# Letting the second pair of sequences join an expert loop one visit later, with its steps spread wider

## What is computed

```python
x = _layernorm(x + attention(x, wq, bq, wk, bk, wv, bv, wo, bo))   # 16 heads of 16
x = _layernorm(x + recurrence(x, ctx_1024, w, u))                  # a decaying scan over the 128 tokens
x = _layernorm(x + experts(x, Wg, W1, b1, W2, b2))                 # 8 experts, 256 -> 1024 (gelu) -> 256
```

## Time and profile before

| | us |
|---|---|
| median of 3 runs (lowest, highest) | 917.84 (917.34, 917.88) |
| profiled execution, its own time | 918.12 |
| span of the trace | 916.4 |
| TensorE busy | 876.4 (96% of the span) |
| VectorE busy | 586.0 (64%) |
| ScalarE busy | 576.5 (63%) |
| mean granted TensorE clock | 0.988 of full speed |
| DMA engines, mean rate | 202 GB/s |

### The profile page before, as it was taken

The page is one execution under the profiler, slowest core; times in us unless marked ns, Lnnn a source line. Parts: engine busy times, 40 slices in busy tenths (PEclk is TensorE's granted clock), DMA queues, the critical chain, the costliest instruction groups (busy, mean ns, idle before and its releaser), DMA issues.

```text
span 916.4 us, 17611 instructions
## 1 busy us (share of the span) xinstructions
PE 876.4 (96%) x6547; PEld 797.0 (87%) x6547; DVE 586.0 (64%) x1197; ACT 576.5 (63%) x969; POOL 80.4 (9%) x116
## 2 busy tenths in 40 slices
PE   6898888999999999999999999999999999999997
PEld 6788787889888999989988889889999889999997
DVE  6779798767656576665565674665676564333574
ACT  7568686766667455776557465765557665444684
POOL 4220012001010011000120010200120000000000
PEclk9999899999999999999999999999999999999999
DMA  8459999997738854686548954497537855665340
GB/s 250 154 191 338 352 311 312 285 301 244 240 109 244 242 174 132 178 231 212 174 127 230 235 169 146 134 231 239 181 118 181 250 183 169 190 187 177 103 139 12
DMA packets 195379, 185.00 MB, mean 202 GB/s; under 512 B 61896, under 2 KB 161504, under 8 KB 195296
## 3 DMA queue, kind: packets, MB, share of 16 engines
q1 hardware_dynamic: 195296, 183.88, 66.6%
HBM read 135.60 MB, written 35.65 MB: 187 GB/s over the span
## 4 chain that ended last, share of the span: by engine, by line
PE 76%; ACT 9%; DVE 5%; issue 2%; DMA 2%; SPq 1%; POOL 1%; POOLq 0%; ACTq 0%; DVEq 0%
PE down_ps L823 11%; PE down_ps L824 11%; PE down_ps L825 11%; PE up_ps L562 11%; PE up_ps L564 11%; PE up_ps L563 11%; DMA pt_lo<-p_lo 2%; ACT h_all L971 2%; PE bank L609 1%; ACT probs L912 1%; PE bank L584 1%; ACT L971 1%; PE bank L562 1%; PE bank L564 1%; PE bank L563 1%
## 5 line engine op out<-in xcount | busy, mean ns | idle before, releaser
L971 ACT ACTIVATE h_all<-up_ps,b_all 128x512 f32<-128x512 f32 (+1 forms) x296 | 182.3, 631 | 259.1 <-PE up_ps L564 250.0
L823 PE MATMUL down_ps<-w_hi,h_hi 128*128 128x256 f32 x1024 | 294.4, 288 | 4.4 <-DVE acc L1252 4.4
L1051 DVE TENSOR_TENSOR h_lo<-h_all,h_hi 128x512 fp32r<-128x512 f32 x256 | 176.3, 691 | 191.1 <-ACT h_hi L962 190.5
L824 PE MATMUL down_ps<-w_lo,h_hi 128*128 128x256 f32 x1024 | 289.8, 283 | 0.0
L825 PE MATMUL down_ps<-w_hi,h_lo 128*128 128x256 f32 x1024 | 289.7, 283 | 0.0
L562 PE MATMUL up_ps<-x2t_hi,w_hi 128*128 128x512 f32 (+1 forms) x588 | 220.1, 374 | 3.7 <-DVE x2t_lo L1051 1.9
L564 PE MATMUL up_ps<-x2t_hi,w_lo 128*128 128x512 f32 (+1 forms) x588 | 215.4, 366 | 0.0
L563 PE MATMUL up_ps<-x2t_lo,w_hi 128*128 128x512 f32 (+1 forms) x588 | 214.7, 365 | 0.0
L823 PEld LDWEIGHTS down_ps<-w_hi,h_hi 128*128 128x128 f32 x1024 | 195.1, 190 | 12.9 <-issue 3.0
L824 PEld LDWEIGHTS down_ps<-w_lo,h_hi 128*128 128x128 f32 x1024 | 195.9, 191 | 7.0
L825 PEld LDWEIGHTS down_ps<-w_hi,h_lo 128*128 128x128 f32 x1024 | 195.8, 191 | 0.0
(11 more groups left out here) (213 smaller groups left out, 953.9 us busy)
## 6 DMA issues: line engine op xcount, KB each, us to landing
w_hi<-w_parts SPq DMA_DIRECT2D x200, 256.0 KB, 3.3
w_lo<-w_parts SPq DMA_DIRECT2D x200, 256.0 KB, 3.5
w_raw<-in_w_dram SPq DMA_DIRECT2D x96, 256.0 KB, 4.1
w_parts<-w_hi SPq DMA_DIRECT2D x64, 256.0 KB, 4.0
w_parts<-w_lo SPq DMA_DIRECT2D x64, 256.0 KB, 4.2
x_in<-in_x_dram SPq DMA_DIRECT2D x8, 256.0 KB, 4.1
ctx_sb<-in_ctx_dram SPq DMA_DIRECT2D x8, 256.0 KB, 3.8
out_dram<-acc SPq DMA_DIRECT2D x8, 256.0 KB, 2.3
```

What stands on the lines that cost most here:

```text
L823: nc.tensor.matmul(ps, hi, w2h[:, c, :], start=c == 0 and j == 0, stop=False, skip_group_check=True)
L824: nc.tensor.matmul(ps, hi, w2l[:, c, :], start=False, stop=False, skip_group_check=True)
L971: a = nc.scalar.activation(h_all[:, unit % HALL, k * wide:(k + 1) * wide], up_ps[unit % 2][:, k * wide:(k + 1) * wide], ACT.Gelu_apprx_tan ...
L1051: return nc.vector.tensor_tensor(dst, src, hi.bitcast(F32), ALU.subtract)
```

## The change

Two tables of numbers. Joins move from (0, 5, 9, 13, ...) to (0, 6, 10, 14, ...), so that there are 38 visits instead of 37. The single visits are now 0 to 5, 8 and 9, and the last four; the number of items stays 512. The second pair has 8 more items before it joins and its steps are spread over them. The third pair still joins at item 92, but begins 8 items later. Steps of the later pairs keep their items.

```diff
-JOIN = (0, 5, 9, 13, 17, 21, 25, 29)
+JOIN = (0, 6, 10, 14, 18, 22, 26, 30)
...
 EARLY = [
-    {E_0: 3, E_1: 3, X_BIAS: 6, T_0: 7, T_1: 8, W_0: 10, W_1: 11, S_2: 13, M_2: 13, S_3: 13, M_3: 13, E_2: 15, E_3: 15, T_2: 17, T_3: 18, W_2: 20, W_3: 21,
-     ATT: 22, CTX: 22, WO: 23, NORM1: 25, Y1: 26, XEXP: 26, REC_0: 27, REC_1: 28, REC_2: 29, REC_3: 29, BACK: 31, NORM2: 32, R_TURN: 34,
...
+    {E_0: 3, E_1: 3, X_BIAS: 7, T_0: 8, T_1: 9, W_0: 12, W_1: 13, S_2: 15, M_2: 15, S_3: 15, M_3: 15, E_2: 18, E_3: 18, T_2: 20, T_3:
+     21, W_2: 24, W_3: 25, ATT: 27, CTX: 27, WO: 28, NORM1: 30, Y1: 32, XEXP: 32, REC_0: 33, REC_1: 34, REC_2: 35, REC_3: 35, BACK: 38,
+     NORM2: 39, R_TURN: 42, R_LOGITS: 44, R_MAX: 45, R_GATE: 49, R_GATE_T: 53, R_BIAS: 55},
```

More of the change, by code:

```diff
@@ L1424 @@
 EARLY = [
-    {E_0: 3, E_1: 3, X_BIAS: 6, T_0: 7, T_1: 8, W_0: 10, W_1: 11, S_2: 13, M_2: 13, S_3: 13, M_3: 13, E_2: 15, E_3: 15, T_2: 17, T_3: 18, W_2: 20, W_3: 21,
-     ATT: 22, CTX: 22, WO: 23, NORM1: 25, Y1: 26, XEXP: 26, REC_0: 27, REC_1: 28, REC_2: 29, REC_3: 29, BACK: 31, NORM2: 32, R_TURN: 34,
[L1427 to L1431, removed]
+    {E_0: 3, E_1: 3, X_BIAS: 7, T_0: 8, T_1: 9, W_0: 12, W_1: 13, S_2: 15, M_2: 15, S_3: 15, M_3: 15, E_2: 18, E_3: 18, T_2: 20, T_3:
+     21, W_2: 24, W_3: 25, ATT: 27, CTX: 27, WO: 28, NORM1: 30, Y1: 32, XEXP: 32, REC_0: 33, REC_1: 34, REC_2: 35, REC_3: 35, BACK: 38,
+     NORM2: 39, R_TURN: 42, R_LOGITS: 44, R_MAX: 45, R_GATE: 49, R_GATE_T: 53, R_BIAS: 55},
+    {X: 33, X_LOW: 34, X_BIAS: 35, QK: 37, K_COPY: 37, Q_COPY: 37, K_LOW: 38, Q_LOW: 40, DIAG_0: 41, V: 40, V_ADD: 43, V_SPLIT: 44,
+     S_0: 46, M_0: 46, S_1: 46, M_1: 46, DIAG_1: 48, E_0: 49, E_1: 49, T_0: 51, T_1: 53, S_2: 56, M_2: 56, S_3: 56, M_3: 57, W_0: 60,
+     E_2: 60, E_3: 60, W_1: 61, T_2: 62, T_3: 64, W_2: 67, W_3: 69, ATT: 71, CTX: 72, WO: 73, NORM1: 75, Y1: 77, XEXP: 77, REC_0: 77,
+     REC_1: 78, REC_2: 79, REC_3: 80, BACK: 84, NORM2: 85, R_TURN: 87, R_LOGITS: 89, R_MAX: 90, R_GATE: 91, R_GATE_T: 95, R_BIAS: 97}]
 LAG = 3
```

## The result

The changed kernel takes 922.85 us (median of 8 runs, 920.11 to 927.51), the kernel before 917.86 in the same session: a ratio of 1.0052, 95% interval 1.003 to 1.0073. It is **slower by 0.5%**, where 913.5 us was forecast, in a range up to 920.5.

What follows compares the result with a forecast made beforehand. The prediction took TensorE as the bound nearly everywhere, with VectorE's backlog making it wait and full DMA engines right behind in the single visits. Its eight terms summed to -4.3 us, from 918.1 to a median of 913.5 us, range 907 to 920.5.

Steps and rivals of the forecast that it cites:

- term 6: Third pair: W_2 and W_3 come too close behind T_2 and T_3 for their transposes, +1.1 us (0 to 2.2).
- the first rival: Single visits: DMA engines take the gain, or full VectorE only moves its waits; 917.4 us, no difference; chance 0.19.
- Term 8: Single visits, items 10 to 49: DMA needs 5.9 us from slack, mostly held by 8.3 us in hand; +2.0 (0 to 6.6).
- the second's: Rival: late kept copies delay the third pair's transposes, W_3 waits 8.2 us and a dip follows; 921 us, chance 0.18.
- Term 5: Two 2.0 us waits of down items for `acc`: unchanged at the join, gone at visit 5's end, -2.0 (0 to -2.0).
- Term 3: After the second pair's ATT wait: the 5.6 us clock dip to 0.50 goes, -2.5 us (0 to -2.5).
- term 2: Second pair's ATT: TensorE's 4.0 us wait falls to 1.2, -2.8 us (bounds -1.4 and -4.0).
- term 4: BACK: its 1.7 us wait for `mix` nearly goes with one more item between, -1.3 us (0 to -1.7).
- term 7: Visits 8 and 9: reads of kept weights may make TensorE wait anew, +0.5 us (0 to 3).
- Term 1: One double visit becomes two single ones with more, narrower matmuls on TensorE, +0.7 us.

Runs made afterwards that it cites:

- all_three: Changed kernel with kept copies and reads halved, third pair's W_2 and W_3 at items 68 and 71, BACK and NORM2 at 82 and 83: 914.62 us, 0.9959.
- before_half: Kernel before with every kept copy and every read of a kept part cut to half its columns: ratio 0.9992 to the kernel before.
- after_half: Changed kernel with kept copies and reads cut to half their columns: ratio 0.9997 to the kernel before.
- spaced: Changed kernel, full copies, third pair's W_2 and W_3 at 68 and 71, REC_3 at 80, BACK at 83, NORM2 at 84: 918.43 us, 1.0002.
- after_w23: Changed kernel with the third pair's W_2 and W_3 at items 68 and 71, ATT to REC_3 up to two items later: 921.07 us, 1.0034.

## Why the prediction was wrong

**The sum, in three parts.** The forecast was -4.3 us, the measured +0.52% are +4.8. The halved and spaced versions split the difference of 9.1, each part good to some 2 us:

| part | forecast | measured | from |
|---|---|---|---|
| terms 1 to 5, the later joins and the wider spacing | -7.9 | -3.0 | `all_three` less `before_half` |
| term 6 and what it left out, the third pair's table | +1.1 | +3.5 | `after_half` less `all_three` |
| terms 7 and 8, the DMA traffic | +2.5 | +4.3 | changed kernel less `after_half`, less the 0.7 that halving gives the kernel before |

The largest miss is in the first part.

**Terms 2 to 5 were counted whole.** They took 8.6 us off, as if a wait that goes were time won. In `all_three`, with the traffic halved and the third pair spaced, waits are only 3.0 and the clock 1.0 below the kernel before. ATT gave 2.2 and one wait for `acc` 2.0. The wait of the join for `x2t_lo`, put at 0, went from 1.9 to 0.5. Against that `xt_lo` (projections) is waited for 1.4 more, gelu 1.0 and BACK 1.0, and a wait of 1.0 for `x` (L1237) is new. From 80.1 to 156.2 us VectorE is busy for 67.8 of 76.1 us there, against 63.8 in the halved kernel before. This is near what the first rival said in its last sentence, that VectorE only moves its waits; that its fullness is the cause is argued, not shown.

**Term 8 and the rivals.** The step that failed here is "That holds the 5.9, though not at each piece: +2.0"; the traffic cost 4.3. The slack of one piece, 8.3 us, was taken for that of all. It wasn't: other pieces had 2.5 and 5.3 in hand already before, in the changed kernel the copies were up to 12 us late, and ScalarE waited for them 12.2 us in all. Of the changed kernel's ledger, the halved one lacks 2.3 us of gelu's wait, 2.0 of the join's, 0.7 of the transposes' and 3.6 of clock, 8.6 us together, in an execution that was 4.7 above the median. That ScalarE's splits would wait for copies was the first rival's mechanism, and copies that delay the transposes the second's, at 0.18 and 921 us; it measured 922.85. That 921 is near is luck in part. The point against it, that slower items would give the transposes time, was true only in part: the wait for `pt_lo` was 4.1 us, not 8.2, and the rest came through gelu and the join, which it didn't have.

**Term 5.** The wait at the end of the double visit went, as forecast. The one at the join was put at 0 change ("the same steps around it now") and grew by 2.0. ScalarE there waited 3.7 us for a copy, and VectorE got its pieces late. The halved kernel has it at 2.0, so that the growth goes with the traffic.

**Term 6** had mechanism and sign right: +1.1 forecast; 3.4 us of wait with halved copies, 4.1 in full. It went wrong by taking half the bound, and even the bound of 2.2 was too low.

**A term was missing.** Pairs leave at the end of visit 7, and that end moved from item 90 to item 82, in front of BACK and NORM2. The additions, the moments and R_TURN's late `x2`, on VectorE after the change:

```profile
228.78 1.65 DVE L1252 SCALAR_TENSOR_TENSOR acc<-down_ps,gate,acc 128x256 f32<-128x256 f32 x4
230.46 0.75 DVE L1057 BATCH_NORM_STATS2 stats<-acc 128x6 f32<-128x256 f32 x2
...
235.18 1.53 DVE L1068 TENSOR_SCALAR x<-y,moments,rstd 128x256 f32<-128x256 f32 x2 [0.86 <-POOL rstd L1339]
```

2.4 us of wait and a dip of the clock. The prediction said of the added work at this place that VectorE has room, which is true of its share and not of the order.

**Term 3 was a half.** The dip after ATT went, but dips follow waits wherever they are: 3.9 us before, 8.0 after. A new wait of 2 us or more should have carried such a price with some chance, and the ledger shows that this is nearly half of the difference.

**What held.** In the changed kernel's own trace, term 2 (1.8 us of wait left, 1.2 forecast), term 4 (no wait of BACK, 0.4 forecast) and term 7 (no wait for a read in visits 8 and 9). Term 1, +0.7, has no run of its own.

**A check that would have helped.** I read "item 50 near 164 us" as a gain to come. By item 36 the changed kernel was 10.4 us ahead (`h_hi` of that item at 132.2 instead of 142.6), and by item 49 only 1.6. In the halved kernel the lead at item 36 was 12.9 us, and it won nothing in the end either. My reading: most of such a lead is work put off, since the third pair's steps begin eight items later, and isn't time won. What agreed with the time was the sum of the ledger.

**What stays open.** Whether the kept copies or the reads of visits 8 and 9 make up the traffic's part was not tried apart; no wait for a read shows in any trace. Why a wait of 2 us is followed by a dip in one execution and not in another stays open.

## What to carry to other kernels

Before work is moved into a stretch, ask each resource that is full there whether its reserve is per piece or per stretch. Here a queue at 350 GB/s that nobody waited for had little to give, and one slack measured at one place wasn't its budget. And a wait that a table takes away can come back elsewhere: here less than half of the waits and dips that were counted as gone was time won. When a table moves the end of a stage, list what hangs on that end (here additions, norms, stores), as well as the steps that were moved by hand. And compare two schedules by the sum of all waits plus what the lower clock costs, not by how early a given item is reached.

## What the runs showed of the hardware

A wait of TensorE costs more than its length where the granted clock falls behind it: after 4.0 us, 5.6 us at 0.50, 2.5 us lost (before); after 3.3 us, some 6 at 0.50 (after). Waits of 1.3 and 1.5 us in `spaced` were followed by none. In between it went either way: 1.9 us were followed by 7.2 us at 0.53 (`before_half`, 137 us), while 2.7 us in `spaced` (166 us) and 2.4 in `after_w23` (232 us) were followed by a clock of 1.00. Over the thirteen kernels the loss to the lower clock up to item 98 was 2.8 to 8.0 us, in one execution each. The runs of one kernel spread as widely (917.2 to 920.5 us before, 920.1 to 927.5 after); that the dips make this spread isn't shown.

The DMA engines moved 361 GB/s over 38 us of mixed copies and raw reads, with a share of 1.04; 374 GB/s in one slice of 23 us was the highest. The prediction took 351 as the best sustained rate. The rule of the Trainium skill that it quoted ("DMA: Bandwidth & Descriptors", Where 436 GB/s comes from), about 358 GB/s a core between DRAM and SBUF, is within 1% of the first; the one slice stands 4% above it. So the figure isn't a ceiling for this kernel, which runs on one core.
